# A two-layer kernel: layer 1's opening for the first batch moved into layer 0's last quad and tail

## The reference: what is computed

```python
x = x + tanh(g_xattn[0]) * L0_xattn(layernorm(x), ctx, ...)   # 16 heads of 16, keys: 512 context + 512 own
x = x + tanh(g_ffn[0])   * L0_ffn(layernorm(x), ...)
x = x + tanh(g_xattn[1]) * L1_xattn(layernorm(x), ctx, ...)   # 16 heads of 64, keys: 1 null + 512 context
x = x + tanh(g_ffn[1])   * L1_ffn(layernorm(x), ...)          # 8 experts, top 2
```

```python
q = split_heads(x @ Wq) * 64 ** -0.5
k, v = split(ctx @ Wkv);  k, v = split_heads(k), split_heads(v)
k, v = concat(null_k, k), concat(null_v, v)
out = softmax(q @ k.T) @ v          # per head
out = merge_heads(out) @ Wout
out = norm(out) * ln_scale + ln_bias
```

## Time and profile before

| | us |
|---|---|
| median of 3 timed runs | 1991.82 |
| lowest and highest | 1984.52, 1995.12 |
| profiled execution, its own time | 1975.94 |
| span of the profiled execution, first to last instruction | 1974.2 |
| PE busy in the span | 1784.5 |
| DVE busy | 1222.2 |
| ACT busy | 1118.3 |
| mean granted TensorE clock, share of full | 0.971 |

### The profile page before, as it was taken

One profiled execution on the slowest core, in us unless ns is written; L12 is line 12 of the kernel. 1 busy time (PEld: TensorE's weight loads), 2 busy tenths in 40 slices (PEclk: granted clock), 3 DMA queues, 4 the chain that ended last, 5 costly groups with the idle time before them and its releaser, 6 DMA issues. The chain is left out here.

```text
span 1974.2 us, 28140 instructions
## 1 busy us (share of the span) xinstructions
PE 1784.5 (90%) x9516; PEld 1115.6 (57%) x9516; DVE 1222.2 (62%) x2860; ACT 1118.3 (57%) x2332; POOL 459.7 (23%) x434
## 2 busy tenths in 40 slices
PE   5899998997998489999998999899997889999997
PEld 3455554554543234444544354444444889999997
DVE  4868777777783546444456465634654896666664
ACT  2466666666667145545455455544554667666674
POOL 3010210110110100000000002000011677777775
PEclk9899999999999699999999999999999999999999
DMA  3000000000000490000000000100005567776770
GB/s 96 1 22 1 11 12 1 1 22 1 1 1 1 156 352 16 1 22 1 1 1 22 0 1 17 39 1 0 12 23 163 163 181 218 217 204 192 205 212 6
DMA packets 123055, 128.12 MB, mean 65 GB/s; under 512 B 10913, under 2 KB 118305, under 8 KB 122913
## 3 DMA queue, kind: packets, MB, share of 16 engines
q1 hardware_dynamic: 113584, 117.36, 19.0%
q0 software_dynamic: 8160, 8.67, 2.4%
q10 hardware_dynamic: 1168, 0.30, 0.1%
HBM read 97.43 MB, written 30.69 MB: 65 GB/s over the span
## 5 line engine op out<-in xcount | busy, mean ns | idle before, releaser
L857 DVE TENSOR_REDUCE l_tile_max<-psum 128x1 f32<-128x512 f32 x512 | 342.0, 688 | 105.8 <-PE psum L580 104.3
L718 ACT ACTIVATE l_probs<-psum 128x1024 f32<-128x1024 f32 x256 | 248.3, 1022 | 97.1 <-PE psum L592 93.6
L2319 POOL TENSOR_TENSOR moe_w_lo<-moe_w,moe_w_hi 128x512 fp32r<-128x512 f32 x184 | 259.4, 1410 | 117.8 <-ACT moe_w_hi L2101 116.0
L580 PE MATMUL psum<-l_kT,l_qT 128*128 128x512 f32 x512 | 237.2, 471 | 40.4 <-DVE l_tile_max L857 37.1
L1631 DVE TENSOR_REDUCE l_row_max<-psum 128x2 f32<-128x1024 f32 x128 | 156.4, 1222 | 176.6 <-PE psum L1270 175.8
L1471 ACT ACTIVATE l_null_p<-l_s_null,l_neg_max 128x1 f32<-128x1 f32 x256 | 73.8, 288 | 288.9 <-DVE l_neg_max L1633 288.9
L2031 PE MATMUL psum<-moe_xs_hi,moe_w_hi 128*128 128x256 f32 x736 | 211.4, 287 | 1.6 <-DVE moe_xs_lo L2151 1.6
L2031 PE MATMUL psum<-moe_xs_lo,moe_w_hi 128*128 128x256 f32 x736 | 209.2, 284 | 0.0
L2031 PE MATMUL psum<-moe_xs_hi,moe_w_lo 128*128 128x256 f32 x736 | 209.0, 284 | 0.0
L580 PEld LDWEIGHTS psum<-l_kT,l_qT 128*128 128x128 f32 x512 | 98.1, 192 | 131.6 <-DVE l_tile_max L857 111.0
L1473 ACT ACTIVATE l_probs<-psum,l_neg_max 128x512 f32<-128x512 f32 x256 | 171.7, 671 | 0.0
(11 more groups left out here) (299 smaller groups left out, 3309.0 us busy)
## 6 DMA issues: line engine op xcount, KB each, us to landing
moe_w<-in_moe_w SPq DMA_DIRECT2D x276, 256.0 KB, 4.6
moe_sorted_x<-l_zeros SPq DMA_DIRECT2D x1, 17680.0 KB, 57.0
moe_xs<-moe_sorted_x SPq DMA_DIRECT2D x23, 272.0 KB
moe_w<-in_ctxT SPq DMA_DIRECT2D x4, 1024.0 KB, 5.8
moe_w<-in_wkv SPq DMA_DIRECT2D x2, 2048.0 KB, 18.3
x_resid<-in_x SPq DMA_DIRECT2D x4, 512.0 KB, 10.7
l_raw<-in_ctx SPq DMA_DIRECT2D x4, 512.0 KB, 3.6
l_v_raw<-in_ctx SPq DMA_DIRECT2D x4, 512.0 KB, 3.6
```

What stands on the lines that cost most here:

```text
L580: nc.tensor.matmul(bank(max_bank(m)), qT[:, q % SLOTS, h, t * P:(t + 1) * P], kT[:, q % SLOTS, h // 2, half * BANK:(half + 1) * BANK], sta ...
L718: nc.scalar.activation(probs[:, n % PT_RING], wide(2 * (n % 2)), ACT.Exp, scale=SCALE).then_inc(exp_done, 1)
L857: nc.vector.reduce_max(tile_max[:, q % 2, t, h, half:half + 1], bank(max_bank(m)), AX_X).then_inc(max_read, 1)
L2319: nc.gpsimd.tensor_tensor(w13_lo[:, k % SPLITS], w13[:, slot_k, :, cols], w13_hi[:, k % SPLITS].bitcast(F32), ALU.subtract).then_inc(w13_s ...
```

## The change

The opening leaves `layer1` and becomes a class `Opening`, whose pieces `layer0` calls: the statistics of x for batch 0 in the last steps of quad 14; norm, transposes, first queries, first keys, null scores and the scores of token tile 0 in the steps of quad 15; the rest between the pieces of the tail. `layer1`'s loop begins at group 0. The fourth piece of values is computed in the tail too, and no longer in group 0.

To make room, buffers share space. `w_qkv`, `raw`, `v_raw`, `xn`, `xT`, `q_stack` of layer0 now lie in the ring that layer1's weights are loaded into; `k_stack` shares with layer1's `rows` and `xT`, `kT` and `qT` with layer1's `probsT`, `v_sb`, `wo`, `probs` of even groups, and with rounded weights of `experts`. The loads of weights and context are issued by SP in layer0, behind two waits; the small loads, which ACT issued, are issued by SP just ahead of them. The fills of the tail use two banks in turn (7 and 6) where they used six (0 to 5), which are given to the opening.

```diff
+    FILLS = (("xT", 0, 0), ("xT", 0, 1), ("q", 0), ("k", 0), ("null", 0), ("q", 1), ("v", 0, 0, 0), ("v", 0, 0, 1),
+             ("v", 0, 0, 2), ("v", 0, 0, 3), ("k", 1))
+    BANKS = (4, 5, 4, 5, 4, 0, 2, 3, 4, 5, 1)
+    S_BANKS = (4, 0, 2, 4)
...
+    def transpose_tokens(self, pe, c):
+        pe.wait_ge(self.xn_ready, self.s.TT)
...
+    def values(self, pe, kt):
+        s = self.s
+        if kt == 0:
+            pe.wait_ge(self.wv_loaded, 16)
+            pe.wait_ge(self.exp_done, 3)
+        if kt == 2:
+            pe.wait_ge(self.exp_done, 4)
...
-    START_BANKS, TAIL_BANKS, FIRST_BANKS = (MISC, O_BANK), (0, 1, 2, 3, 4, 5), (4, 5, 0, 1, 2, 3)
+    START_BANKS, TAIL_BANKS, FIRST_BANKS = (MISC, O_BANK), (MISC, O_BANK), (4, 5, 0, 1, 2, 3)
...
+                opening.load_small(sp, dram)
+                sp.wait_ge(misc_act, read_no["q", NQ - 1, 1])
+                sp.wait_ge(v_ready, NQ)
+                opening.load_weights(sp, dram)
...
+                def open_second(kt):
+                    if kt == 1:
+                        pe.wait_ge(max_read, MAXES * NQ)
+                        opening.transpose_tokens(pe, 0)
+                        opening.transpose_tokens(pe, 1)
+                    if kt == 2:
+                        opening.project_queries(pe, 0)
+                    if kt in (3, 4):
+                        opening.project_keys(pe, 0, kt == 4)
+                    if kt == 5:
+                        opening.null_scores(pe)
+                    if kt == 6:
+                        opening.scores(pe, 0)
...
                 weigh_values(NQ - 1, KT - 1)
+                tail(0, 0)
                 pe.wait_ge(exp_done, 2 * NQ * KT)
-                pe.wait_ge(max_read, MAXES * NQ)
-                for at in sorted(slots):
-                    if at[0] == TAIL:
-                        fill(at)
+                opening.scores(pe, 1)
+                tail(1, 0, 1)
+                opening.scores(pe, 2)
+                opening.scores(pe, 3)
+                tail(2, 0, 1)
+                opening.project_queries(pe, 1)
+                opening.values(pe, 0)
+                opening.values(pe, 1)
+                tail(3, 0, 1)
+                tail(4, 0)
+                opening.values(pe, 2)
+                opening.values(pe, 3)
+                opening.project_keys(pe, 1, False)
+                tail(5, 0, 1)
+                opening.project_keys(pe, 1, True)
...
+                    if (q, kt) == (NQ - 1, 1):
+                        opening.read_by_scalar(act, ("xT", 0, 0))
+                    if (q, kt) == (NQ - 1, 2):
+                        opening.read_by_scalar(act, ("q", 0))
+                opening.exponentials(act, 0)
                 keep_sums(NQ - 1)
...
+                    if q == NQ - 2 and kt >= 5:
+                        if kt == 5:
+                            chain["second"] = opening.statistics(dve)
+                        next(chain["second"])
...
+                    if kt == 0:
+                        dve.wait_ge(misc_psum, fill_no["k", NQ - 1, 3] + 1)
+                        opening.norm_tokens()
...
                 normalize(NQ - 1)
+                for t in range(1, T):
+                    opening.maxima(dve, t)
                 for h in range(2):
                     add_attention(B - 1, h)
...
                 norm_rows2(B - 1)
+                for t in range(T):
+                    opening.normalize(dve, t)
...
-                for i in range(-3, GROUPS):
+                for i in range(GROUPS):
```

More of the change, by code:

```diff
@@ L685, in fill, with tail @@
                     last.then_inc(misc_psum, 1)
+                def open_second(kt):
[11 more added lines that the diff above has]
+                        opening.scores(pe, 0)
+                def tail(i, *ys):
+                    for y in ys:
+                        fill((TAIL, i, y))
                 for q, kt in steps:
@@ L694, in _ @@
                     fill((q, kt, 0))
+                    if q == NQ - 1:
+                        open_second(kt)
                     for m in ahead[2:3]:
@@ L797, in _ @@
                             unit(b - 1, i)
-                keep_sums(NQ - 1)
[L799 to L804, removed]
+                    if (q, kt) == (NQ - 1, 1):
[3 more added lines that the diff above has]
+                opening.exponentials(act, 0)
+                keep_sums(NQ - 1)
+                for c in range(s.DC):
+                    read_fill((TAIL, 1, c))
+                for t in range(1, T):
+                    opening.exponentials(act, t)
+                opening.read_by_scalar(act, ("q", 1))
+                for t in range(2):
+                    opening.read_by_scalar(act, ("v", 0, 0, t))
+                for c in range(s.DC):
+                    read_fill((TAIL, 3, c))
+                read_fill((TAIL, 4, 0))
+                for i in range(8):
+                    unit(B - 1, i)
+                for t in range(2, 4):
+                    opening.read_by_scalar(act, ("v", 0, 0, t))
             @block.gpsimd
@@ L1017, in _ @@
                     add_ffn(B - 1, h)
+                opening.read_by_vector(dve, ("k", 1))
 class Stream:
@@ L1082, in layer1 @@
     slots = {}
-    for i in range(-3, GROUPS):
+    opening = g["opening"]
+    slots.update({(-1, n, 0): fill for n, fill in enumerate(opening.FILLS)})
+    for i in range(GROUPS):
         b, p = divmod(i, PAIRS)
@@ L1089, in layer1 @@
         if b >= 1 and p == 0:
-            late[0] = ("null_probs", b - 1)
-        if b >= 0 and p == 0:
-            late[1] = ("v", b, 0, 3)
+            late = {0: ("null_probs", b - 1), 1: ("v", b, 0, 3)}
         if b >= 1 and p in (1, 2):
@@ L1294, in values @@
                 def values(b, half, kt):
-                    if b == 0 and half == 0 and kt == 0:
-                        pe.wait_ge(wv_loaded, 16)
                     for c in range(s.CC):
@@ L1472, in exponentials @@
                                              bias=neg_max[:, t, j:j + 1], scale=-1.0)
-                        last = nc.scalar.activation(probs[:, i % 2, t, j, :], bank(2 * (t % 2) + j), ACT.Exp,
+                        last = nc.scalar.activation(probs[i % 2][:, t, j, :], bank(2 * (t % 2) + j), ACT.Exp,
                                                     bias=neg_max[:, t, j:j + 1], scale=SCALE,
```

415 lines of the change are left out of this document (289 added, 126 removed).

## The result

| | before | changed kernel |
|---|---|---|
| median of the timed runs, us | 1993.16 (4 runs) | 1942.74 (4 runs, 1937.99 to 1948.12) |
| ratio, 95% interval | 1 | 0.9754 (0.9725 to 0.9783) |
| profiled execution, own time | 1975.94 | 1948.12 |
| its span | 1974.2 | 1946.4 |
| mean granted clock | 0.971 | 0.972 |

The forecast was 1947. I therefore cut both traces at five events that each of them has, and compare stretch by stretch. ("Copy of sums" is ACT's copy of the bank into which a quad's weighing adds.)

A forecast was written before the change was run, and what follows sets the result against it. PE bounds both layers; between them two chains, one behind the other, leave the engines mostly free. 41.4 us up to group 0 plus 3.4 in it give 44.9; 1991.8 - 44.9 = 1946.9 us, range 1935 to 1961.

The forecast's parts named there:

- Last quad: Layer0's quad 15 with the inserted pieces: PE waits 2.7 us for the norm; copy of sums 12.5 us later.
- Tile 0's exponentials: On ACT ahead of the last quad's copy of sums: cost 0.5 us, bounds 0 and 1.7.
- Rival B: Inserted pieces lengthen both chains more than they fill; PE misses ACT in last quad: gain 25 to 38 us, chance 0.15.
- Tail, first half: From the copy of sums to the feed-forward's transposes: maxima cost nothing, PE late by 0.8, shift 14.6 us.
- Tail, second half: From the feed-forward's transposes to group 0: full clock, 4.1 us to the input product's copy, group 0 at 679.7.
- Group 0: Its last round loses its piece of values: 6.53 becomes 3.09, a gain of 3.4 us.
- No other round changes: In layer1's loop, only group 0's last round gets shorter; all other rounds keep their time.
- Loads: Issued by SP after quad 15's queries are copied: all in the ring near 595, first reader at 620.
- rival C: The weights land late and PE stands in the last quad's step 2: time within 0.5%, chance 0.03.
- rival D: The wait in the last quad's step 1 keeps the clock low: costs 51 us, time 1998, chance 0.04.
- The sum: 41.4 us up to group 0's first product plus 3.4 in group 0: a gain of 44.9 us.
- rival A: The replayed order holds as worked out, over last quad, tail and group 0: gain 40 to 49 us, chance 0.75.

The follow-up runs named there:

- c1: The kernel before, unchanged, run again for a second profile: 1992.74 us, ratio 1.0006 to itself.
- e5: Changed kernel with the norm ahead of DVE's two units in quad 15's step 0 and the token transposes behind step 1's weighing: 1943.67 us, ratio 0.9727 to before.
- e6: As e5, and ACT takes tile 0's exponentials behind the copy of quad 15's sums: 1943.13 us, ratio 0.9744 to the kernel before.
- e3: Changed kernel with the last quad's pieces kept in place, but the tail's pieces run after the tail: 1972.2 us, ratio 0.9898 to the kernel before.
- c2: The changed kernel, unchanged, run again: 1939.98 us, ratio 0.9730 to the kernel before.
- e1: Changed kernel with its buffers and early loads, but all pieces of the opening behind layer0's last addition: 1976.21 us, ratio 0.9944 to the kernel before.
- e2: As e1, with the loads also held back until layer0's last addition to x: 1986.86 us, ratio 0.9988 to the kernel before.
- e4: Changed kernel with DVE's statistics in steps 0, 1 and 3 of quad 14 and the norm in its step 7: 1943.93 us, ratio 0.9770 to before.
- c3: The changed kernel, unchanged, run once more: 1941.96 us, ratio 0.9770 to the kernel before.
- e7: e5 again, unchanged: 1938.55 us, ratio 0.9743 to the kernel before.

## Why the prediction was right

**Last quad, forecast 12.5 us, measured 13.55.** The wait for the norm was there, for the reason given, but 3.96 us instead of 2.7. Set against the copy of quad 14's sums, the norm was done 0.3 us later than forecast (the statistics, costed at nothing, ended at 619.24, and DVE's two units behind them began 0.4 later), and PE was there 0.8 us earlier: I had read its arrival from rows that stand in the fall of the clock of the earlier trace rows. And the clock fell behind the wait, which I had priced at 2.0 us and left out: 0.9 for the transposes and 0.7 for the weighing. These 2.9 us became 1.05 because other things were cheaper. In c1 the same step of the kernel before holds two waits for ACT, 0.48 and 0.18 us:

```profile
619.31 0.74 PE L592 MATMUL psum<-l_qT,l_kT 128*128 128x512 f32 x2 [0.48 <-ACT l_probs L718]
620.22 0.74 PE L592 MATMUL psum<-l_qT,l_kT 128*128 128x512 f32 x2 [0.18 <-ACT l_probs L718]
```

Set beside c1, from the start of one weighing to the next, the account closes. Step 1 took c1 3.72 us (617.17 to 620.89) and the changed kernel 4.94 (624.31 to 629.25). That is 1.22 more, though it holds 1.8 us of queries and a weighing 0.7 longer: some 1.3 us of c1's step, the waits for ACT and what hangs on them, are gone. The two halves of the keys added 1.73 and 1.70 us, the null scores 1.70 and the scores 0.88, 0.5 less than forecast together. In the first profile of before the fall of the clock stood in the place of c1's waits: from copy to copy that quad took 19.82 us, in c1 19.85. So the 12.5 came near the measured 13.55 partly by luck: a wait and a dip put too low stand against a saving that the forecast did not have.

Tile 0's exponentials cost 0.4 (e5 to e6), forecast 0.5. Rival B's idle time of PE in steps 2 to 6 did not come: PE went without a wait from 626 to 649.

**Tail, first half.** Sums to the transposes of the result: 2.51 us (forecast 2.4); to the projection 5.42 (5.6); from there to the feed-forward's transposes 12.14 (12.3). DVE's maxima cost nothing: ahead of the second addition DVE was idle for 0.84 us, for PE's projection. PE was late for the norm by 0.7 (norm done 667.82, transposes 668.50), forecast 0.8.

**Tail, second half.** The full clock came: 3.92 us from the transposes to the copy of the input product (forecast 4.1, before 6.54). The four normalizations ended at 673.2, 5.5 us as estimated, ahead of the first unit at 673.99. Units took 8.20 us from that copy (8.18). Then 5.03 us to group 0's first product, where I had 4.8. From sums to there 34.71 against 35.0. e3 shows the mechanism by itself: without the pieces the same transposes are back at 1.94 us.

**Group 0, forecast 3.4.** It lost 3.03 to 3.06 us in the traces of the changed kernel; a wait of PE of 0.44 us for ACT's copy of the queries (at 691.07) is what is missing to 3.4. Behind it the step is smaller than it looks: the eight rounds of groups 1 and 2 take 39.6 us in the changed kernel's three traces, 38.8 in both of before. PE now waits there too, once, for ACT's copy of the queries, where before it had no wait; I take it that the piece of values that is gone had given ACT time to catch up, which no run tests by itself (timeline of c2):

```profile
705.53 1.98 PE L1584 MATMUL psum<-moe_w 128*128 128x512 f32 x4 [0.53 <-ACT l_qk L1771]
```

So this term of the sum should have been 2.2 us. "No other round changes" was wrong by 0.8: the shift is there up to 109 us behind group 1's first product (108.6 in both traces of before, 109.4 in the three of the changed kernel, at the same wait for ACT). Farther on the profiles of one kernel differ from each other by more than that.

**Loads.** They were issued from 577.64 on; no wait in the last quad names a DMA, so rival C fell. e1 against e2 shows what the sum had only implied: 8.95 us of the gain come from weights that are there before the chain.

**The clock, rival D.** It fell for about 4 us and came back, so D fell. The Trainium skill (TensorE: Matmul & The Clock Gate, Part 1: The HAM clock gate) has activity restore the clock. The trace agrees: 0.55 from 624 to 626 us with PE busy, 1.00 from 626 to 628 and in the filled tail.

**Rival B's price.** It was added up wrongly: 2 to 6 us for the dips, with 1.7, 1.5 and 5, are 10 to 14 us and not 10 to 20, so its gain should have read 31 to 35 us. What was measured doesn't hang on it.

**The sum.** Traces give 40.7 or 43.7 us up to group 0, by the profile of before taken, plus 3.05, less 0.8: 43 to 46 against 44.9. Over all executions the mean falls from 1990.3 (61, standard error 0.7) to 1942.1 (16, 1.0), by 48.2. Some 2 to 5 us of that I can't place: they would lie at the start or behind group 1, where two and three traces vary by more than that. This stays open. So the mechanism and its terms held, but the time, 1942.7, lies 4.2 below the forecast, which no term of the sum explains; by the two medians the gain is 50.4 us, above the 40 to 49 of rival A; by the means it lies within it.

## What to carry to other kernels

Two latency chains of independent work, one behind the other, are worth interleaving, and the gain is where the engine that is the bound elsewhere idles: the tail's pieces gave 27 us, the pieces put into PE-bound steps 6. Such a change can be forecast within some us by replaying the new order from rows of the old trace, if the rows are not taken from within a fall of the clock, and if the result is compared between events that both traces have, not by spans. Work moved ahead to remove a wait pays only where the new place has slack on its own engine: in e4 it had none.

## What the runs showed of the hardware

A wait of PE of 3.96 us at a clock of 1.00 was followed by 4 us at 0.55 to 0.60 in the profiled execution, and in c2 and c3 the transposes and the weighing behind the same wait took 1.88 and 1.87, 1.74 and 1.94 us. In e5 and e7 waits of 0.78 and 0.43 at that place left the clock at 1.00. In e4 a wait of 2.42 us was enough: the clock was 0.98 in the 3 us with it and 0.50 in the 2 us behind. Shorter lulls differ from profile to profile: the last steps of quad 14 hold waits of 1.33 to 1.35 and 0.18 us in all thirteen profiles, and the weighing behind them took 1.93 us in the profile of before (the fall of the earlier trace rows), 1.55 in e4, and 1.06 or 1.07 in the other eleven, c1 among them.

The same kernel's time varies with the clock, by 12.5 us over 16 executions (1937.99 to 1950.44); the granted clock of the single executions in c3 was 0.977 or 0.978 for 1938.59 to 1939.31 us, and 0.971 or 0.972 for 1944.61 to 1950.44. So a saving of 4 us is below what a handful of executions can tell, even where the traces repeat the stretch to 0.05 us.
